# One of a segment's 32 blocks of exps on VectorE instead of ScalarE, in an adaLN block with differential attention

## The reference

```
x: [4, 2048, 256]
h = layernorm(x) * (1 + ca) + sa
q, k = h Wq, h Wk     # 32 heads of 8;  v = h Wv: 16 heads of 16
aw = softmax(q k^T / sqrt(8))          # 32 maps of 2048 x 2048 for each batch
aw = aw[head, 0] - lam * aw[head, 1]   # 16 differences
attn = rmsnorm(aw v) * subln_w * (1 - lambda_init)
x = x + ga * (attn Wo)
h = layernorm(x) * (1 + cb) + sb
x = x + gb * (h ternary(Wf)^T)
```

## Time and profile before

| | |
|---|---|
| time, median of 3 runs | 3913.02 us (3913.0 to 3917.55) |
| the profiled execution: time | 3916.22 us |
| the profiled execution: span | 3914.5 us |
| ScalarE busy | 97% of the span |
| TensorE busy, granted clock | 96%, 0.993 |
| VectorE busy | 30% |
| GpSimd busy | 16% |
| exps of the attention | 4096, the first begun at 108.3 us, the last at 3868.9 us |

### The profile page before, as it was taken

The page is one execution under the profiler, slowest core; times in us unless marked ns, Lnnn a source line. Parts: engine busy times, 40 slices in busy tenths (PEclk is TensorE's granted clock), DMA queues, the critical chain, the costliest instruction groups (busy, mean ns, idle before and its releaser), DMA issues.

```text
span 3914.5 us, 75013 instructions
## 1 busy us (share of the span) xinstructions
PE 3750.6 (96%) x32110; PEld 960.2 (25%) x32110; DVE 1188.5 (30%) x2745; ACT 3797.7 (97%) x4168; POOL 628.2 (16%) x402
## 2 busy tenths in 40 slices
PE   6899999999999999999999999999999999999997
PEld 4222212122222222222222222222222222211122
DVE  7222223123233232233333233232332223211133
ACT  3899999999999999999999999999999999999995
POOL 5111212012021211212012121211211011011011
PEclk9999999999999999999999999999999999999998
DMA  7221121111212221122121212221112111201101
GB/s 245 52 57 26 46 39 49 41 33 48 52 44 47 60 49 42 46 45 60 45 53 48 59 35 47 60 49 42 46 35 50 31 41 23 51 3 26 36 20 41
DMA packets 132413, 188.27 MB, mean 48 GB/s; under 512 B 11100, under 2 KB 107100, under 8 KB 132064
## 3 DMA queue, kind: packets, MB, share of 16 engines
q1 hardware_dynamic: 131248, 182.53, 19.0%
q10 hardware_dynamic: 816, 0.79, 0.1%
HBM read 97.61 MB, written 85.47 MB: 47 GB/s over the span
## 4 chain that ended last, share of the span: by engine, by line
ACT 58%; issue 29%; PE 11%; DVE 1%; POOL 1%; SPq 0%; DMA 0%; ACTq 0%; POOLq 0%; DVEq 0%
ACT probs L736 58%; PE ps L851 5%; PE ps L837 3%; PE ps L763 1%; PE ps L771 1%; PE ps L757 0%; DVE normed L1021 0%; SPq L381 0%; PE ps L821 0%; SPq L420 0%; DMA v_scr<-a_v 0%; DMA a_x<-in_x_dram 0%; DVE seg_t L1141 0%; POOL a_rest L641 0%; POOL probs L647 0%
## 5 line engine op out<-in xcount | busy, mean ns | idle before, releaser
L736 ACT ACTIVATE probs<-ps 128x1024 f32<-128x1024 f32 x4096 | 3759.2, 1506 | 12.2 <-PE ps L837 11.4
L851 PE MATMUL ps<-probs,values 128*32 128x512 f32 x16384 | 2183.1, 605 | 8.6 <-DVE seg_t L1141 4.0
L837 PE MATMUL ps<-queries,keys 64*128 64x512 bf16 x8192 | 1467.0, 385 | 104.1 <-DMA queries<-wmod_sb 10.0
L675 POOL TENSOR_TENSOR seg_rs<-seg_ms,neg_half 64x16 f32<-64x16 f32 x128 | 370.2, 2893 | 2860.4 <-DVE seg_ms L1150 2860.4
L837 PEld LDWEIGHTS ps<-queries,keys 64*128 64x128 bf16 x8192 | 375.2, 92 | 1841.5 <-ACT probs L736 1586.6
L851 PEld LDWEIGHTS ps<-probs,values 128*32 128x32 f32 x16384 | 322.4, 108 | 568.9 <-issue 496.4
L1141 DVE STREAM_TRANSPOSE seg_t<-ps 128x512 f32<-128x512 f32 x128 | 91.8, 717 | 848.5 <-PE ps L851 848.5
L1127 DVE TENSOR_TENSOR e_tmp<-ps,e_gate 128x512 f32<-128x512 f32 x64 | 44.1, 689 | 451.8 <-PE ps L763 451.8
L1154 DVE TENSOR_TENSOR seg_n<-seg_d,seg_rs 64x256 f32<-64x256 f32 x128 | 61.9, 483 | 386.3 <-POOL seg_rs L675 386.3
L1104 DVE TENSOR_SCALAR a_qk<-ps 128x512 f32<-128x512 f32 x48 | 33.2, 692 | 341.2 <-PE ps L771 341.2
L1158 DVE SCALAR_TENSOR_TENSOR seg_a<-seg_n,subln_sb 32x256 f32<-32x256 f32 x256 | 131.5, 514 | 6.1
(11 more groups left out here) (143 smaller groups left out, 1231.0 us busy)
## 6 DMA issues: line engine op xcount, KB each, us to landing
queries<-q_scr SPq DMA_DIRECT2D x62, 384.0 KB
keys<-k_scr SPq DMA_DIRECT2D x62, 384.0 KB
v_scr<-a_v SPq DMA_DIRECT2D x16, 1024.0 KB, 4.6
values<-v_scr SPq DMA_DIRECT2D x31, 512.0 KB
q_scr<-a_parts SPq DMA_DIRECT2D x28, 384.0 KB, 2.6
k_scr<-a_parts SPq DMA_DIRECT2D x28, 384.0 KB, 2.6
a_x<-in_x_dram SPq DMA_DIRECT2D x16, 512.0 KB, 12.9
attn_scr<-seg_o SPq DMA_DIRECT2D x128, 64.0 KB, 1.7
```

Of the source, the lines that this page charges most:

```text
L675: nc.gpsimd.tensor_tensor(seg_rs[:, :], seg_ms[:, :], neg_half[0:64, :], ALU.pow).then_inc(seg_rs_done, 1)
L736: nc.scalar.activation(probs[:, u % PRING, n % PAIRS, :, :], slots[slot_of(body, n)], ACT.Exp).then_inc(exp_done, 1)
L837: last = nc.tensor.matmul(slots[slot_of(body, n)][:, half, :], keys[buf][at:at + KS_ROWS, n % PAIRS, blk * P:(blk + 1) * P], queries[buf][ ...
L851: last = nc.tensor.matmul(pv[j:j + VW, :], values[buf][:, blk, half, :], probs[:, u % PRING, pair, half, :], start=(blk == 0), stop=(blk = ...
```

## The change

In every segment but the first of each batch (124 of 128) VectorE computes block 15, which is the second block of unit 7 (`D_UNIT`); ScalarE leaves it out. VectorE clamps and scales the scores out of PSUM into `d_y` (this frees the slot, `d_read`), rounds them to a quarter of an exponent step by adding and subtracting a large number, subtracts, turns the rounded part into a power of two through an integer write, and evaluates a polynomial in four nested steps of `scalar_tensor_tensor`. Both blocks of unit 7 have a tile of their own, `d_probs`, so the ring of four units is one of the others.

The nine instructions, each on 128x1024, stand in VectorE's order in pieces: three in unit 6, two in unit 7, one in each of units 8 to 11. TensorE leaves the product of unit 7 out in unit 9 and does it behind that of unit 13 (`D_BEHIND`), in unit 15, when it also waits for `d_done`. `scores` of block 18 wait for `d_read` in place of an exp. The three tiles of the gates become one, `gates`, which the rounded part uses once the gates are stored, and VectorE waits once for that store.

```diff
+    def summed(unit):
+
+        k, u = divmod(unit, NB)
+        if shared(k) and D_UNIT <= u <= D_BEHIND:
+            u = D_BEHIND if u == D_UNIT else u - 1
+        return k * NB + u + 1
...
                 for n in range(2 * BODY):
-                    u = n // PAIRS
+                    unit = body * BODY + n // PAIRS
+                    if shared_block(body * (2 * BODY) + n):
+                        continue
...
-                pe.wait_ge(exp_done, body * (2 * BODY) + n + 1)
+                before = body * (2 * BODY) + n - SLOTS
+                if shared_block(before):
+                    pe.wait_ge(d_read, shares_below(before) + 1)
+                else:
+                    pe.wait_ge(exp_done, SLOTS + exps_below(before + 1))
...
                         if u >= LAG:
-                            weighted(body, u - LAG)
+                            if not shared_unit(body * BODY + u - LAG):
+                                weighted(body, u - LAG)
+                            if (u - LAG) % NB == D_BEHIND and shared(body * SEGS + u // NB):
+                                weighted(body, u - LAG - D_BEHIND + D_UNIT)
...
+            def share_read(k):
+
+                n = k * (PAIRS * NB) + PAIRS * D_UNIT + 1
+                dve.wait_ge(scores_ready, n + 1)
+                V.tensor_scalar(d_y[:, :], slots[n % SLOTS].rearrange("p h c -> p (h c)"), EXP_LOW, QUARTER_LOG2E, ALU.max, ALU.mult).then_inc(d_read, 1)
+                dve.wait_ge(d_read, SHARES[k] + 1)
+                link = share_link(k, 0)
+                link.then(V.tensor_scalar(d_n, d_y[:, :], ROUND, -ROUND, ALU.add, ALU.add))
+                link.then(V.tensor_tensor(d_y[:, :], d_y[:, :], d_n, ALU.subtract))
...
+            def share_powers(k):
+                link = share_link(k, 2)
+                V.tensor_scalar(d_n.bitcast(mybir.dt.int32), d_n, BIAS, 2.0 ** 25, ALU.add, ALU.mult)
+                link.then(V.scalar_tensor_tensor(d_out, d_y[:, :], POLY[4], d_y[:, :], ALU.add, ALU.mult))
+
+            def share_term(k, i):
+                share_link(k, 6 - i).then(V.scalar_tensor_tensor(d_out, d_out, POLY[i], d_y[:, :], ALU.add, ALU.mult))
+
+            def share_last(k):
+                V.scalar_tensor_tensor(d_out, d_out, POLY[0], d_n, ALU.add, ALU.mult).then_inc(d_done, 1)
...
+                        share(body * SEGS + u // NB, u % NB)
```

More of the change, by code:

```diff
@@ L13 @@
 P = 128
+POLY = [0.7355579137802124, 2.0393989086151123, 2.827145576477051, 2.613037347793579, 1.8219317197799683]
+LEAD = 1.3595123291015625
+BIAS = (126.0 + LEAD) / 4.0
+ROUND = 1.5 * 2.0 ** 21
+QUARTER_LOG2E = float(np.log2(np.e) / 4.0)
+EXP_LOW = -87.0
 ONE_PAIR = float(np.array([0x3F803F80], np.uint32).view(np.float32)[0])
@@ L139, in adaln_diff_attention, with shared, shared_unit, shared_block @@
     S_LINKS, E_LINKS, P_LINKS = 7, 6, 4
+    D_UNIT, D_BEHIND, D_LINKS = 7, 13, 6
+    ALL_SEGS = B * GP * SEGS
+    def shared(k):
+        return k % (GP * SEGS) > 0
+    SHARES = [sum(shared(j) for j in range(k)) for k in range(ALL_SEGS + 1)]
+    def shared_unit(unit):
+        return shared(unit // NB) and unit % NB == D_UNIT
+    def shared_block(n):
+        return n >= 0 and shared_unit(n // PAIRS) and n % PAIRS == 1
+    def shares_below(n):
+        if n <= 0:
+            return 0
+        k, at = divmod(n, PAIRS * NB)
+        return SHARES[k] + (shared(k) and at > PAIRS * D_UNIT + 1)
+    def exps_below(n):
+        return n - shares_below(n)
+    RING = [u for u in range(ALL_SEGS * NB) if not shared_unit(u)]
+    RING_AT = {u: r for r, u in enumerate(RING)}
+    def summed(unit):
[3 more added lines that the diff above has]
+        return k * NB + u + 1
     TAIL_E = [(NC - 2, i) for i in range(len(E_LAST[-1]), E_STEPS)] + [(NC - 1, i) for i in range(E_STEPS)]
@@ L277, in place_of, with probs_of @@
             return (s % 2, s // 2) if body == LAST else (s // NC, s % NC)
+        def probs_of(unit):
+            return d_probs if shared_unit(unit) else probs[:, RING_AT[unit] % PRING, :, :, :]
         aux = ps[:, 7, :]
@@ L361, in adaln_diff_attention @@
         seg_stored = sem("seg_stored")
+        d_read = sem("d_read")
+        d_chain = sem("d_chain")
+        d_done = sem("d_done")
         block = ctx.enter_context(nc.Block())
@@ L846, in weighted @@
                     pe.wait_ge(pv_read, body * SEGS + seg + 1)
-                pe.wait_ge(exp_done, SLOTS + body * (2 * BODY) + PAIRS * (u + 1))
+                unit = body * BODY + u
+                pe.wait_ge(exp_done, SLOTS + exps_below(PAIRS * (unit + 1)))
+                if shared_unit(unit):
+                    pe.wait_ge(d_done, SHARES[unit // NB] + 1)
                 for pair in range(PAIRS):
@@ L850, in weighted @@
                         j = 32 * (2 * pair + half)
-                        last = nc.tensor.matmul(pv[j:j + VW, :], values[buf][:, blk, half, :], probs[:, u % PRING, pair, half, :],
+                        last = nc.tensor.matmul(pv[j:j + VW, :], values[buf][:, blk, half, :], probs_of(unit)[:, pair, half, :],
                                                 start=(blk == 0), stop=(blk == NB - 1))
@@ L1132, in e_evacuate, with share_link, share @@
                     norm_apply(e_x2, e_rstd, e_rstd_done, job, e_normed)
+            def share_link(k, first):
+                return Chain(dve, d_chain, SHARES[k] * D_LINKS + first)
+            def share_read(k):
[6 more added lines that the diff above has]
+                link.then(V.tensor_tensor(d_y[:, :], d_y[:, :], d_n, ALU.subtract))
+            d_out = d_probs[:, 1, :, :].rearrange("p h c -> p (h c)")
+            def share_powers(k):
[6 more added lines that the diff above has]
+                V.scalar_tensor_tensor(d_out, d_out, POLY[0], d_n, ALU.add, ALU.mult).then_inc(d_done, 1)
+                dve.wait_ge(d_done, SHARES[k] + 1)
+            def share(k, u):
+                if not shared(k):
+                    return
+                if u == 6:
+                    share_read(k)
+                elif u == 7:
+                    share_powers(k)
+                elif u in (8, 9, 10):
+                    share_term(k, 11 - u)
+                elif u == 11:
+                    share_last(k)
             def segment(body, s):
```

16 lines of the change are left out of this document (11 added, 5 removed).

## The result

The changed kernel took 3939.1 us (median of 4, 3935.6 to 3940.9) against 3914.6 us (4 runs, 3913.0 to 3917.6). The ratio is 1.0061, 95% interval 1.0043 to 1.0078: slower by 24.6 us, between 17 and 31 by the interval, where 19.8 were forecast. The profiled execution of after took 3935.6 us, span 3933.8, which is 19.3 us more than the span of before. It is the shortest of its four runs, as the profiled one of before is near the top of its own.

What follows compares the result with a forecast made beforehand. ScalarE's exp rate was taken as the bound, TensorE within half a block of it for most of the time. Saving 113.7 us, minus costs 40.6, 37.9, 21, 13, 15 and 6, gave +19.8: 3933 us, range 3892 to 3970.

Steps and rivals of the forecast that it cites:

- E: Nineteen segments of turns and last body, margins near nothing: evacuations behind the share, second product among pieces, +15 us (0 to 30).
- A: Block 16's scores can't come earlier on TensorE, so ScalarE waits 0.92 us less the margin: +40.6 us.
- B: The second product in unit 15 stands ahead of block 32's scores, costing 0.89 us less the margin: +37.9 us.
- C: The share's result is 1.3 us late for unit 15 in 16 segments with layernorm work between: +21 us.
- D: Read late three times behind a long evacuation in unit 6; block 18's scores wait 4.3 us each: +13 us.
- F: GpSimd's projection split slows VectorE's share in 24 segments, 2.35 us falling on it, 0.25 late: +6 us (0 to 38).
- The reading of the margins: An exp's surplus over 1.02 us is how much later its scores could come unnoticed: 0.41, 0.62 or 0.84 us.
- (1): TensorE keeps up: margins only show how early ScalarE begins, A and B vanish: 3854 us, chance 0.05.
- (2): A and B stand, but the share is shorter, with C, E and F at lower ends: 3891 us, chance 0.10.
- (3): In between, with C and E at half: between 3905 and 3921 us, chance 0.17.
- (4): Share starved, longer than its 15.5 us window in most segments: 4008 us, or 3950 to 3970 with one cause; chance 0.14.
- (5): The change does not do what it says: block 15 stays on ScalarE; chance nil.

Runs made afterwards that it cites:

- x3: Changed kernel with VectorE's share cut to the read from PSUM; unit 7's product, still in unit 15, takes the first block's exps without waiting: 3898.3 us.
- x4: Changed kernel with no share on VectorE: ScalarE skips block 15, unit 7's product is in unit 9 with the first block's exps twice: 3848.3 us.
- x8: Changed kernel without the share in segments 60, 92 and 123, where the long evacuation stands ahead of the read: 3925.6 us.
- x5: Changed kernel without the share in 19 segments with margins near nothing (27 to 30, 59 to 63, 91 to 95, 123 to 127): 3907.7 us.

## Why the prediction was right, step by step

The forecast was 3933 us (+19.8), the measurement 3939.1 (+24.6; +19.3 between the two profiled spans). The waits below are the gaps between the ends of consecutive exps less 0.9166 us, summed by block number over all segments of the profiled executions. They sum to 142.7 us after and 7.1 before, 135.5 more, against 113.7 us of exps saved: 21.9 by these, of which the two ends of the program take 2.6 back. The tight segments are the nineteen of E. Term by term (us):

| term | forecast | by the waits |
|---|---|---|
| A, block 16 | 40.6 | 43.1 |
| B and C, a segment's first block | 58.9 | 62.6 (x3: 39 and 23.5) |
| D, the late read, block 18 in three segments | 13 | 12.3 |
| what follows D at later blocks | - | 1.9 |
| E, blocks 17 to 31 of the other tight segments | 15 | 12.1 |
| F, all other waits | 6 | 3.5, of it 3.1 at block 20 |
| sum | 133.5 | 135.5 |


- **The reading of the margins** was right for the kernel before: there the exps of the unit behind a piece begin 0.04 us after the end of their scores, so that their surplus over 1.02 us is TensorE's lead. It isn't a general rule. In the changed kernel block 14 beside a projection takes 1.18 us, a surplus of 0.16, and yet the wait at block 16 is 0.51 us and not 0.76: the lead is still the 0.41 of before, and the surplus, set back to nothing at the last wait, hasn't grown up to it. The forecast took the surplus from the right kernel.
- **A, forecast 40.6:** the waits at block 16 sum to 43.5 (0.4 before). By kind 0.51, 0.30 and 0.08 us, to the hundredth what the margins gave; the rest is the turns'. x4 has them at 43.3 with everything else removed.
- **B, forecast 37.9, and C, forecast 21:** the waits at a segment's first block sum to 63.8 (1.2 before), 62.6 where 58.9 were forecast; x3 splits them into 39 and 23.5. Beside a projection B is 0.45 us (0.48 was forecast; product to piece takes 0.86), beside a transpose 0.24 (0.27), without a piece mostly under 0.03 (0.05). Of C, TensorE waited 17.7 us in 18 waits for the share's last instruction. A segment of that kind, a long evacuation between the share's halves:

```profile
1434.95 0.69 DVE L1217 TENSOR_SCALAR gates<-d_y 128x1024 f32<-128x1024 f32 x1
...
1441.54 1.38 DVE L1094 TENSOR_SCALAR normed<-e_x,moments,e_rstd 128x256 f32<-128x256 f32 x4 [1.12 <-POOL e_rstd L682]
1442.84 0.68 DVE L1224 TENSOR_SCALAR gates<-gates 128x1024 int32<-128x1024 f32 x1
...
1448.46 1.23 DVE L1231 SCALAR_TENSOR_TENSOR wmod_sb<-wmod_sb,gates 128x1024 f32<-128x1024 f32 x1
1449.83 1.06 PE L921 MATMUL ps<-wmod_sb,values 128*32 128x512 f32 x8 [0.92 <-DVE wmod_sb L1231]
```

  The late result costs TensorE 0.92 us there, not 1.3, and the next segment's first block comes 1.14 us later than in x3. The share itself is right to 0.1 us: 1.22 for the read, 1.23 for each nested step, 0.69 for both others, the integer write too.
- **D, forecast 13:** three waits of 4.2 us for the read, 12.3 us for ScalarE. The term lacked what follows, 1.9 us in all, where the clock is lower for a while (last section). The 15.6 us of x8 hold A and B of these segments too.

```profile
1882.09 1.38 DVE L1094 TENSOR_SCALAR normed<-e_x,moments,e_rstd 128x256 f32<-128x256 f32 x4 [1.12 <-POOL e_rstd L682]
1883.39 1.21 DVE L1214 TENSOR_SCALAR d_y<-ps 128x1024 f32<-128x1024 f32 x1
...
1884.66 1.46 PE L904 MATMUL ps<-queries,keys 64*128 64x512 bf16 x6 [4.17 <-DVE d_y L1214]
...
1885.31 1.02 ACT L799 ACTIVATE probs<-ps 128x1024 f32<-128x1024 f32 x1 [4.05 <-PE ps L904]
```

- **E, forecast 15,** an estimate between wide bounds, so that its size is in part luck. The waits give 12.1. Of these 8.2 are in segments 30, 62 and 94, behind block 18, where the steps of the bounds stand: TensorE waited there for VectorE's work on two of them, as the term said, and no such row stands in the kernel before:

```profile
PE ps L871 <- DVE wmod_sb L1321: 5.0, 3, 1.7
...
PE ps L871 <- DVE m_worst L1316: 3.3, 3, 1.3
```

  (us in all, times, the longest). 1.6 of the 8.2 goes with a fall of the clock in segment 94. A and B take 21.3 us in all tight segments, by C's late results too, where 17.4 were saved. x5 less x8, 17.9 us, holds this difference beside E, so it isn't E by itself.
- **F, forecast 6:** the share does take longer beside GpSimd, and none of it reached unit 15. In a segment whose split meets the share, the six later instructions take from 1322.16 to 1330.54, 8.4 us, against 6.9 in the fence above (1442.84 to 1449.69):

```profile
1322.16 0.94 DVE L1224 TENSOR_SCALAR gates<-gates 128x1024 int32<-128x1024 f32 x1
1323.02 1.62 DVE L1225 SCALAR_TENSOR_TENSOR wmod_sb<-d_y 128x1024 f32<-128x1024 f32 x1
1324.68 4.59 DVE L1228 SCALAR_TENSOR_TENSOR wmod_sb<-wmod_sb,d_y 128x1024 f32<-128x1024 f32 x3
...
1322.62 0.95 POOL L676 CAST a_parts<-a_rest 128x512 bf16<-128x512 f32 x1
1323.65 2.02 POOL L677 TENSOR_TENSOR a_parts<-a_rest,a_parts 128x512 bf16<-128x512 f32 x1
```

  That is 1.5 us of delay with 2.1 to spare. The step that failed is the 2.35 taken for it; GpSimd's own last instruction took 2.02 for 1.22. The rule of the Trainium skill (SBUF — State Buffer, Who interferes with whom) is borne out in kind: both engines stretch while they overlap. In size it isn't: by the rule all 3.7 us might have fallen on the share, and 1.5 did. What these segments do pay is a wait of 0.09 to 0.15 us at block 20, about 3 us in all: the evacuation of unit 7 stands behind the share's first three instructions, and in x3, which has only the first of them, these waits are gone.

So the sum was within 5 us because A, B, C and D, which came out of rows, were each within 3 us. By the waits A, B and C were 6.2 too small together and E and F 5.4 too large, and that these cancel is luck. The segments came out as stated: 28.51 us without pieces, and 29.37 to 29.53 with projections in units 7 and 15, the longer ones with a wait at block 20. TensorE's waits for VectorE's share sum to 30 us (17.7 and 12.5), between the 10 and 80 that would have spoken against C to F.

**The rivals.** (1), that the margins mean nothing, falls with x4: 3848 where it wanted 3801 to 3806. (2), a shorter share, and (4), a starved one, fall with the measured durations. What (4) had for it was half right: both sides stretch, but the share doesn't become longer than its window. (3), C and E at half, falls with C at 23.5 and E at 12.1, and (5) with the 3972 exps.

**What stays open.** The medians of the two kernels differ by 24.6 us, the profiled executions by 19.3. The other three runs of the changed kernel have spans 2.8 to 5.4 us above the profiled one. No trace of them exists, so where these 5 us lie isn't shown. Two things on record vary by a good part of it. The first exp of the attention begins at 107.1 us in the profiled execution of the changed kernel and at 108.3 in that of before; over all ten kernels it is 105.9 to 111.0. And the mean granted clock of these three runs is 0.990 where the profiled one had 0.991; in x8 the five runs at 0.993 average 3923.8 us and the five at 0.991 or 0.992 average 3927.2.

## What to carry to other kernels

Work taken off the engine that bounds a kernel was worth at most the lead that the engine feeding it had, as long as that one's order stayed as it was. The trace told the lead without any experiment: how much longer than its least duration an instruction took that may start early. Here it was 0.41, 0.62 and 0.84 us for a block of 0.92, and each share was worth that little before it had cost anything. The reading holds for an instruction that begins as soon as its input is there, in a stretch without waits; behind a wait the durations say nothing of the lead, and the time from the input's end to the start has to be read instead.

Where the second engine has an order written by hand, the move frees a place in that order (a product in unit 9) and takes one elsewhere (unit 15). The freed place belongs ahead of the block that must come earlier, and the new product where no piece follows: the change lost 24.6 us with `D_BEHIND` = 13 and gained 8 with 14, with the same work. With the tight segments left out as well (105 shares) it gained 36, and with the free place two units earlier 50.

## What the runs showed of the hardware that was not expected

A wait of 4.2 us on TensorE costs more than itself. Busy time and granted clock (PEclk) of the changed kernel in stretches around the first late read:

```profile
1870.00:1880.00 10.00, 10.00 (x102) 2.56 (x100) 5.61 (x14) 9.49 (x11) 2.89 (x1) 1.00 0.25 83
1880.00:1884.60 4.60, 0.49 (x8) 0.00 (x0) 3.41 (x12) 1.26 (x2) 1.01 (x1) 0.85 0.20 65
1884.60:1888.00 3.40, 3.07 (x16) 0.58 (x16) 3.30 (x5) 2.69 (x3) 0.00 (x0) 0.50 0.00 0
1888.00:1892.00 4.00, 4.00 (x30) 0.60 (x24) 3.90 (x4) 3.64 (x5) 0.00 (x0) 0.75 0.00 0
```

The columns are busy us and instructions of PE, PEld, DVE, ACT, POOL, then the granted clock. It stood at its full level (2.4 GHz) until the wait; TensorE was busy 0.49 of 4.6 us; then it was 0.50 (1.2 GHz), from 1883 to about 1890. The first product behind the wait took 1.93 us where 1.06 is usual:

```profile
1886.93 1.93 PE L921 MATMUL ps<-probs,values 128*32 128x512 f32 x8
...
1889.76 1.17 PE L921 MATMUL ps<-probs,values 128*32 128x512 f32 x8
```

Behind each of the three late reads the clock was lower for a while, and ScalarE waited 1.9 us more in all at the later blocks of these segments. Late evacuations may be part of these waits; only the slower matmuls are seen in the trace. The kernel before has the full clock in the same stretch. Once it fell without a wait of that size, in the third turn, where ScalarE lost 1.6 us at block 22 that the second turn doesn't show in the same place:

```profile
2905.00:2909.00 4.00, 4.00 (x30) 1.13 (x24) 2.92 (x4) 2.53 (x3) 0.00 (x0) 0.72 0.01 2
```

What TensorE did before that which it didn't do in the second turn was not found. The waits of about 1 us left the clock as it was.

A single long wait isn't needed. In x8, which has no late read, the clock fell to 0.50 three times all the same: at 1001.7, behind waits of TensorE for VectorE of 0.8 and 1.67 us, at 2896.1, behind 1.27 and while one of 1.67 went on, and at 3817.7, behind one of 2.26. TensorE was busy 4.1 of the 6 us ahead of the first and 4.2 of the 6 ahead of the second. ScalarE's waits in these three segments are 1.0 to 1.5 us longer each than in the changed kernel.
